# Linear attention in a decoder layer: reciprocals spread by DMA instead of TensorE, and the block's work in another order

## The chip, the cores and the metric

The kernel runs on one core of a Trainium2 chip. The metric is the device time of one execution in microseconds (us), lower is better. Engines are named as in the profile: PE is TensorE, DVE is VectorE, ACT is ScalarE, POOL is GpSimd, SP is SyncE, which here issues the DMAs.

## What is computed

One layer of a decoder on x of shape (2, 2048, 512): linear attention over x, cross attention over a context of 154 rows, and a mixture of experts, each behind a layer norm and added to x. The change touches the linear attention alone. Its mathematics, cut from the reference:

```
x = x + attn(layernorm(x), w_qkv, proj_matrix, w_out, b_out)
q_proj = elu1(einsum('bhnd,hdf->bhnf', q, proj_matrix))
k_proj = elu1(einsum('bhnd,hdf->bhnf', k, proj_matrix))
kv = einsum('bhnf,bhnd->bhfd', k_proj, v)
attn = einsum('bhnf,bhfd->bhnd', q_proj, kv)
k_sum = k_proj.sum(axis=2)
z = 1.0 / (einsum('bhnf,bhf->bhn', q_proj, k_sum) + 1e-08)
out = (attn * z[..., None]) @ w_out + b_out
```

There are 16 heads of 32 columns. The next step of the layer, the query projection of the cross attention, is made in the same stage.

## The kernel before

Tokens are cut into eight blocks of 512 (NBLK = 8). The kernel has four stages: `project` (keys, values and queries), `attend_linear`, `attend_cross` and `experts`. Only `attend_linear` changes; a DRAM array of `attend_cross` moves to the second half of a larger one.

`attend_linear` is a pipeline over the blocks, written out by hand. Each engine runs `turns(slot)`: for i from -1 to 8 and for the slots s = 0 to 7 it does what its own `slot` function lists, in that order. In turn i three blocks are in work: the features of block i+1 ("ahead", two heads in each slot), the division, output projection and layer norm of block i ("now"), and the cross-attention queries of block i-1 ("behind"). What PE does in a slot after the two heads is in the table `PLAN`:

```
0: [("ND", 3), ("XQ", 0, 0, 12)],
1: [("XQ", 1, 0, 12)],
2: [("R", 0), ("R", 1), ("R", 2), ("R", 3), ("XQ", 2, 0, 12)],
3: [("ND", 0), ("O", 0, 0, 12)],
4: [("O", 1, 0, 12), ("O", 2, 0, 6)],
5: [("ND", 1), ("O", 2, 6, 12), ("O", 3, 0, 12)],
6: [("XQ", 3, 0, 12), ("T", 0), ("T", 1)],
7: [("ND", 2), ("T", 2), ("T", 3)],
```

The jobs are these.
- Head h: one matmul (L1166), ACT relu (L1003) and exp (L1006), and DVE's sum of both (L1086), which makes `qp`, ring of eight. PE may run three heads ahead of DVE (three banks `li_h_bank`).
- ND g: denominators (`p_den`, L1176) and numerators (`p_num`, L1182) of four heads. ACT evicts them to `den` (L960) and `num` (L951).
- Reciprocals: two DVE instructions of half a row each (L1049) write `den[:, 1]`; only 16 of the 128 rows hold different numbers. ACT (L965) and POOL (L924) split the reciprocals into a high and a low half.
- R g: two matmuls (L1191) with a constant matrix `spread` copy the reciprocals of four heads to all their 128 rows, in a PSUM bank. DVE multiplies `num` by it (L1054, `normalise`).
- ACT writes the high half of the normalised heads (L971, `normalised`), and POOL the low half of all four groups (L936). The output projection reads both.
- O t: 12 matmuls (L1204) for 128 tokens. Those of t = 0 go group by group, three matmuls each, and each group waits for its low half (`norm_lo`).
- DVE's `add_out` adds an O to x and takes the statistics (L1060 to L1067), POOL takes the power (L942), DVE's `norm` writes `xn` (L1074), which has two buffers, T t is four transposes of it (L1213), and ACT (L980) and DVE (L1080) evict the high and low halves (`turned`).
- XQ g: 12 matmuls (L1226) of the query projection. ACT writes the high half (L989), DVE the low half (L1091), and SP stores both (L874). `xq` has two buffers.

O, T, XQ and R share three PSUM banks in the order of the jobs: a job waits until the third job before it has been evicted (`bank_free`). XQ 0 waits for all four transposes of its block to be evicted. All DMAs are issued by SP, in the order of its own slots, and a wait on SP holds all DMAs behind it.

## Time and profile before

| | |
|---|---|
| time, median of 3 runs | 2378.44 us (2377.59 to 2380.17) |
| time of the profiled execution | 2380.94 us |
| its span | 2379.2 us, 34267 instructions |
| PE busy | 2278.0 us (96%) |
| DVE, ACT, POOL busy | 1390.5, 1158.5, 838.9 us |
| `project` | 0 to 417 us |
| `attend_linear` | 417 to 743.4 us, PE busy 308.66 |
| `attend_cross` | 743.4 to about 1136 us |
| `experts` | about 1136 us to the end |

The limits of the stages were read off the first and last instructions of each. The page's chain of work that ended last names PE for nearly all of its steps, so a stage is worth what happens to PE in it. A "busy" PE may still be running at half clock; the column PEclk of the views by window gives the granted clock as a share of full speed.

### The profile page before, as it was taken

The page shows a single profiled execution, that of the slowest core. Times are in us where ns is not written, and L with a number is a line of the kernel's source. Part 1 is how long each engine was busy: PE and PEld are TensorE (multiplying, and loading weights), DVE is VectorE, ACT ScalarE, POOL GpSimd, SP SyncE. Part 2 cuts the span into 40 slices and gives each one's busy share as a digit, 9 for nine tenths or more (in the row PEclk, how much of TensorE's full clock was granted, in tenths as well). Part 3 has the DMA queues.
Part 4 walks back from the last instruction along what each step waited for, and adds up shares of the span by engine and source line. Part 5 has one row for each costly group of instructions (what it writes and reads, how often), then busy time and mean ns, then how long its engine had stood idle before and what let it go on. Part 6 is the DMA issues. An engine that isn't in the chain of part 4 may idle for free.

```text
span 2379.2 us, 34267 instructions
## 1 busy us (share of the span) xinstructions
PE 2278.0 (96%) x12200; PEld 1775.7 (75%) x12200; DVE 1390.5 (58%) x2258; ACT 1158.5 (49%) x2745; POOL 838.9 (35%) x820
## 2 busy tenths in 40 slices
PE   7999999899998899998799999999999999999998
PEld 6888886566666566665588878888788887888887
DVE  5555456777774668777644466444664445644444
ACT  3555566767663767774544444333343333433332
POOL 1444345333341245545677762111111111111111
PEclk9999999999999899999899999999999999999999
DMA  7655546666646457784656546454345543464442
GB/s 209 161 146 128 134 107 157 210 187 195 177 142 181 102 145 188 185 225 138 217 174 212 177 141 214 171 177 142 129 153 201 177 142 125 136 215 139 140 139 77
DMA packets 140218, 387.46 MB, mean 163 GB/s; under 512 B 15920, under 2 KB 38064, under 8 KB 123440
## 3 DMA queue, kind: packets, MB, share of 16 engines
q1 hardware_dynamic: 139760, 384.77, 53.9%
q8 instruction: 98, 1.61, 0.3%
q10 hardware_dynamic: 288, 0.49, 0.1%
q14 instruction: 72, 0.59, 0.1%
HBM read 254.00 MB, written 104.07 MB: 151 GB/s over the span
## 4 chain that ended last, share of the span: by engine, by line
PE 51%; DVE 1%; issue 0%; ACT 0%; DVEq 0%
PE ex_pg L2593 32%; PE ex_pd L2609 18%; DVE ex_xb L2410 0%; PE ex_pd L2559 0%; PE ex_pd L2570 0%; DVE ex_up L2430 0%; DVE ex_acc L2447 0%; ACT ex_xb L2260 0%; DVE stage L2406 0%; DVE ex_ht L2439 0%; DVE ex_lg L2348 0%; DVE ex_rank L2382 0%; DVE ex_gt L2379 0%; DVE ex_rank L2380 0%; DVE ex_g L2423 0%
## 5 line engine op out<-in xcount | busy, mean ns | idle before, releaser
L2593 PE MATMUL ex_pg<-ex_xb,first_wg 128*128 128x512 f32 x3360 | 821.5, 391 | 12.0 <-DVE ex_up L2430 7.0
L2593 PEld LDWEIGHTS ex_pg<-ex_xb,first_wg 128*128 128x128 f32 x3360 | 632.0, 189 | 153.0 <-issue 15.7
L2609 PE MATMUL ex_pd<-ex_wd,ex_ht 128*128 128x512 f32 x1920 | 486.4, 389 | 2.9 <-issue 2.6
L2609 PEld LDWEIGHTS ex_pd<-ex_wd,ex_ht 128*128 128x128 f32 x1920 | 360.0, 188 | 79.1 <-issue 4.5
L2447 DVE SCALAR_TENSOR_TENSOR ex_acc<-ex_pd,ex_share,ex_acc 128x512 f32<-128x512 f32 x320 | 239.7, 749 | 302.4 <-PE ex_pd L2609 302.2
L2267 ACT COPY ex_m<-ex_pg 128x512 f32<-128x512 f32 x240 | 141.1, 588 | 383.5 <-PE ex_pg L2593 383.4
L2211 POOL TENSOR_TENSOR ex_h<-ex_g,ex_up 128x512 f32<-128x512 f32 x80 | 103.3, 1292 | 553.3 <-issue 458.2
L1590 ACT ACTIVATE cr_prob<-cr_s_bank,cr_top 128x154 f32<-128x154 f32 x512 | 194.7, 401 | 89.3 <-DVE cr_top L1700 86.6
L422 POOL TENSOR_TENSOR pr_ks_sum<-pr_ks_sum,pr_kp 128x512 f32<-128x512 f32 x128 | 165.2, 1291 | 161.6 <-DVE pr_kp L570 150.0
L2271 ACT ACTIVATE ex_g<-ex_g 128x512 f32<-128x512 f32 x160 | 101.3, 633 | 238.0 <-DVE ex_g L2423 165.5
L2203 POOL TENSOR_TENSOR ex_wd<-stage,ex_wd 128x512 fp32r<-128x512 f32 x80 | 105.8, 1343 | 260.1 <-ACT ex_wd L2248 260.1
L2278 ACT CAST ex_ht<-ex_h 128x512 fp32r<-128x512 f32 x160 | 99.4, 622 | 133.1 <-POOL ex_h L2211 133.0
L570 DVE SCALAR_TENSOR_TENSOR pr_kp<-pr_pk,pr_kp 128x512 f32<-128x512 f32 x128 | 88.5, 691 | 104.1 <-ACT pr_kp L475 103.4
L1700 DVE TENSOR_REDUCE cr_top<-cr_s_bank 128x3 f32<-128x462 f32 x192 | 110.4, 578 | 59.3 <-PE cr_s_bank L1865 59.2
L1865 PEld LDWEIGHTS cr_s_bank<-cr_k_w,cr_q 96*128 96x128 f32 x512 | 74.1, 199 | 77.1 <-issue 37.2
L2416 DVE TENSOR_TENSOR ex_g<-ex_pg,ex_m 128x512 f32<-128x512 f32 x80 | 55.3, 691 | 130.1 <-PE ex_pg L2593 124.9
L2439 DVE TENSOR_TENSOR ex_ht<-ex_h,ex_ht 128x512 fp32r<-128x512 f32 x160 | 122.2, 764 | 0.1
L1865 PE MATMUL cr_s_bank<-cr_k_w,cr_q 96*128 96x154 f32 x512 | 98.5, 302 | 20.1 <-DMA cr_q<-xq_scratch 11.9
L1590 ACT ACTIVATION_READ_ACCUMULATOR cr_prob<-cr_s_bank,cr_top 128x1 f32 x512 | 110.1, 215 | 0.0
L1927 PE MATMUL cr_bank<-cr_wo,cr_u 128*128 128x512 f32 x384 | 103.4, 407 | 4.0 <-DVE cr_x L1729 4.0
L1086 DVE SCALAR_TENSOR_TENSOR qp<-li_h_bank,qp 128x512 f32<-128x512 f32 x112 | 75.2, 681 | 46.7 <-ACT qp L1006 46.0
L473 ACT ACTIVATE pr_kp<-pr_pk 128x512 f32<-128x512 f32 x124 | 73.2, 590 | 52.8 <-PE pr_pk L702 52.8
(222 smaller groups left out, 3588.9 us busy)
## 6 DMA issues: line engine op xcount, KB each, us to landing
first_wg<-w_scratch SPq DMA_DIRECT2D x60, 1024.0 KB, 5.1
first_wg<-w_scratch SPq DMA_DIRECT2D x60, 768.0 KB, 4.3
w_scratch<-first_wg SPq DMA_DIRECT2D x20, 1792.0 KB, 6.8
stage<-in_units SPq DMA_DIRECT2D x60, 512.0 KB, 6.9
qk<-pr_kq SPq DMA_DIRECT2D x192, 128.0 KB, 2.4
qk<-q_scratch SPq DMA_DIRECT2D x96, 256.0 KB, 4.7
cr_q<-xq_scratch SPq DMA_DIRECT2D x96, 256.0 KB, 8.0
q_scratch<-pr_kq SPq DMA_DIRECT2D x128, 128.0 KB, 2.3
```

Source lines behind the costliest of these rows:

```text
L422: nc.gpsimd.tensor_tensor(part, part, slot(step), ALU.add).then_inc(ks_step, 1)
L1590: last = nc.scalar.activation(prob[:, n % 2, t, j, 0:KEYS], s_bank[(MU * n + v) % SBANKS][:, at * KEYS:(at + 1) * KEYS], ACT.Exp, bias=top ...
L1700: nc.vector.tensor_reduce(dst.rearrange("p t j -> p (t j)") if t == t_end else dst[:, :, 0], src, AX.X, ALU.max, negate=True).then_inc(top ...
L1865: mm = nc.tensor.matmul(s_bank[at % SBANKS][:, k * KEYS:(k + 1) * KEYS], q3[:, n % QRING, j, t * P:(t + 1) * P], k_w[:, n // G // BLK, j, ...
L1927: mm = nc.tensor.matmul(bank_of("O", m)[:], u[:, s, g, tile_cols(m)], wo[:, w, g], start=(n == 0), stop=(n == 3 * G - 1))
L2203: nc.gpsimd.tensor_tensor(wd[:, n % 2, LO, cols], d_raw[:, cols], wd[:, n % 2, HI, cols].bitcast(F32), ALU.subtract).then_inc(wd_lo, 1)
L2211: nc.gpsimd.tensor_tensor(h[:, f, 1], g[:, f, 1], up[:], ALU.mult).then_inc(h1_set, 1)
L2267: nc.scalar.copy(dst[:], pg[f][BANK[j]][:]).then_inc(m_set, 1)
L2439: nc.vector.tensor_tensor(ht[:, LO, f, k], h[:, f, k], ht[:, HI, f, k].bitcast(F32), ALU.subtract)\
L2447: nc.vector.scalar_tensor_tensor(acc[:, at], bank_of("D", n, i)[:], share[:, NT * half + at, e:e + 1], acc[:, at], ALU.mult, ALU.add).then ...
L2593: mm = nc.tensor.matmul(pg[f][BANK[j]][:], wg[:, f, j, s, c * P:(c + 1) * P], xb[:, j, m, c * TB:(c + 1) * TB], start=(k == 0 and j in FRESH),
L2609: mm = nc.tensor.matmul(bank_of("D", n, i)[:], ht[:, s, f, k, t * P:(t + 1) * P], wd[:, n % 2, m, f * D:(f + 1) * D], start=(at == 0), sto ...
```

## The change

The diff, without the declarations of semaphores and the renamed arguments:

```diff
-        2: [("R", 0), ("R", 1), ("R", 2), ("R", 3), ("XQ", 2, 0, 12)],
-        3: [("ND", 0), ("O", 0, 0, 12)],
-        4: [("O", 1, 0, 12), ("O", 2, 0, 6)],
-        5: [("ND", 1), ("O", 2, 6, 12), ("O", 3, 0, 12)],
-        6: [("XQ", 3, 0, 12), ("T", 0), ("T", 1)],
+        2: [("XQ", 2, 0, 12)],
+        3: [("ND", 0), ("XQ", 3, 0, 12)],
+        4: [("O", 0, 0, 12), ("O", 1, 0, 6)],
+        5: [("ND", 1), ("O", 1, 6, 12), ("O", 2, 0, 12)],
+        6: [("O", 3, 0, 12), ("T", 0), ("T", 1)],
...
-        spread = sb("spread", [P, G, P], F32R)
-        rec = sb("rec", [P, 2, TB], F32R)
+        rec = sb("rec", [P, G, TB])
-        xq = sb("xq", [P, 2, 2, TB], F32R)
+        xq = sb("xq", [P, G, 2, TB], F32R)
...
+                def spread_rec(i):
+                    sp.wait_ge(recip_set, 2 * (i + 1))
+                    for j in range(HG):
+                        sp.dma_start(rec_dram[i, j * G:(j + 1) * G], den[j * HD:j * HD + G, 1]).then_inc(row_out, 16)
+                    sp.wait_ge(row_out, 16 * HG * (i + 1))
+                    if i:
+                        sp.wait_ge(divided, G * i)
+                    rows = rec_dram[i].rearrange("(j g) t -> j g t", j=HG)
+                    for j in range(HG):
+                        sp.dma_start(rec[j * HD:(j + 1) * HD], rows[j:j + 1].broadcast_to([HD, G, TB])).then_inc(rec_in, 16)
...
-                    if behind and s in (1, 2, 3, 7):
-                        query_out(i - 1, (1, 2, 3, 7).index(s))
+                    if now and s == 1:
+                        spread_rec(i)
+                    if behind and s in (1, 2, 3, 4):
+                        query_out(i - 1, s - 1)
...
-                def reciprocal_low(i, n):
-                    cols = slice(n * TB // 2, (n + 1) * TB // 2)
-                    pool.wait_ge(rec_hi, 2 * i + n + 1)
-                    nc.gpsimd.tensor_tensor(rec[:, LO, cols], den[:, 1, cols], rec[:, HI, cols].bitcast(F32),
-                                            ALU.subtract).then_inc(rec_set, 1)
...
-                def reciprocal_high(i, n):
-                    cols = slice(n * TB // 2, (n + 1) * TB // 2)
-                    act.wait_ge(recip_set, 2 * i + n + 1)
-                    nc.scalar.copy(rec[:, HI, cols], den[:, 1, cols]).then_inc(rec_hi, 1)
...
-                    if m or g >= 2:
-                        act.wait_ge(xq_out[g % 2], 16 * (2 * m + g // 2))
+                    if m and g < 2:
+                        act.wait_ge(xq_out[g], 16 * 2 * m)
...
-                    if now and s == 2:
+                    if behind and s == 2:
+                        query(i - 1, 2)
+                    if behind and s == 3:
+                        query(i - 1, 3)
+                    if now and s == 3:
                         for g in range(G):
                             normalised(i, g)
...
-                    dve.wait_ge(r_full, G * i + g + 1)
-                    nc.vector.tensor_tensor(num[:, g], num[:, g], bank_of(i, "R", g)[:], ALU.mult).then_inc(r_taken, 1)
+                    dve.wait_ge(rec_in, 16 * HG * (i + 1))
+                    nc.vector.tensor_tensor(num[:, g], num[:, g], rec[:, g], ALU.mult).then_inc(divided, 1)
...
+                for landed in xq_out:
+                    pool.wait_ge(landed, 16 * NB * BLK * G // 2)
```

The last two lines are POOL's first in `attend_cross`, ahead of two memsets. `spread_rec` has the form that `attend_cross` already uses for its own reciprocals (L1431 to L1440 of the kernel before). DVE's `reciprocal` of a later block also waits until the rows of the block before have left `den`. The low halves of the normalised heads were all on POOL already, and stay there.

On ACT, the place is turn 1, where the first block with queries behind it is divided: end of slot 2, slot 3. `li_xq` is the eviction of an XQ, `li_u_att` the high half of the normalised heads, and the pairs on `qp` are the heads. Before:

```order
L1006 ACTIVATE qp<-qp 128x512
L971 CAST li_u_att<-li_num 128x512 x4
L989 ACTIVATE li_xq<-li_bank,li_bq 128x512
L1003 ACTIVATE qp<-li_h_bank 128x512
L1006 ACTIVATE qp<-qp 128x512
L1003 ACTIVATE qp<-li_h_bank 128x512
L1006 ACTIVATE qp<-qp 128x512
L951 COPY li_num<-li_p_num 128x512
```

After:

```order
L999 ACTIVATE qp<-qp 128x512
L984 ACTIVATE li_xq<-li_bank,li_bq 128x512
L996 ACTIVATE qp<-li_h_bank 128x512
L999 ACTIVATE qp<-qp 128x512
L996 ACTIVATE qp<-li_h_bank 128x512
L999 ACTIVATE qp<-qp 128x512
L984 ACTIVATE li_xq<-li_bank,li_bq 128x512
L966 CAST li_u_att<-li_num 128x512 x4
L952 COPY li_num<-li_p_num 128x512
```

The four casts to `li_u_att` stood ahead of the eviction of XQ 2, and now stand behind that of XQ 3.

On PE, the same place, slots 2 to 4. `li_rec,li_spread` is R, `li_u_ln,wq` is XQ and `li_wo,li_u_att` is O. Before:

```order
L1166 MATMUL li_h_bank<-qk,f_w 128x512 x2
L1191 MATMUL li_bank<-li_rec,li_spread 128x512 x8
L1226 MATMUL li_bank<-li_u_ln,wq 128x512 x12
L1166 MATMUL li_h_bank<-qk,f_w 128x512 x2
L1176 MATMUL li_p_den<-qp,ks_w 32x512 x4
L1182 MATMUL li_p_num<-qp,kv_w 32x512 x4
L1204 MATMUL li_bank<-li_wo,li_u_att 128x512 x12
L1166 MATMUL li_h_bank<-qk,f_w 128x512 x2
L1204 MATMUL li_bank<-li_wo,li_u_att 128x512 x18
```

After:

```order
L1160 MATMUL li_h_bank<-qk,f_w 128x512 x2
L1211 MATMUL li_bank<-li_u_ln,wq 128x512 x12
L1160 MATMUL li_h_bank<-qk,f_w 128x512 x2
L1170 MATMUL li_p_den<-qp,ks_w 32x512 x4
L1176 MATMUL li_p_num<-qp,kv_w 32x512 x4
L1211 MATMUL li_bank<-li_u_ln,wq 128x512 x12
L1160 MATMUL li_h_bank<-qk,f_w 128x512 x2
L1189 MATMUL li_bank<-li_wo,li_u_att 128x512 x18
```

R is gone, and XQ 3, which stood three slots later, stands directly ahead of the heads and the first O.

On DVE, the end of turn 1: from the last `add_out` to the transposes' evictions. Before:

```order
L1060 TENSOR_TENSOR li_x<-li_x,li_bank 128x512
L1062 BN_STATS li_stats<-li_x 128x6
L1064 COPY li_pause<-half 128x1
L1065 BN_AGGR li_mv<-li_stats 128x2
L1067 TENSOR_SCALAR li_mv<-li_mv 128x1
L1086 SCALAR_TENSOR_TENSOR qp<-li_h_bank,qp 128x512
L1074 TENSOR_SCALAR li_xn<-li_x,li_mv,li_rstd 128x512
L1091 SCALAR_TENSOR_TENSOR li_xq<-li_bank,li_bq,li_xq 128x512
L1086 SCALAR_TENSOR_TENSOR qp<-li_h_bank,qp 128x512
L1074 TENSOR_SCALAR li_xn<-li_x,li_mv,li_rstd 128x512
L1080 TENSOR_TENSOR li_u_ln<-li_bank,li_u_ln 128x4x128 x2
```

After, from the first head of slot 6 (`li_xn` is norm):

```order
L1077 SCALAR_TENSOR_TENSOR qp<-li_h_bank,qp 128x512
L1065 TENSOR_SCALAR li_xn<-li_x,li_mv,li_rstd 128x512
L1077 SCALAR_TENSOR_TENSOR qp<-li_h_bank,qp 128x512
L1065 TENSOR_SCALAR li_xn<-li_x,li_mv,li_rstd 128x512
L1051 TENSOR_TENSOR li_x<-li_x,li_bank 128x512
L1053 BN_STATS li_stats<-li_x 128x6
L1055 COPY li_pause<-half 128x1
L1056 BN_AGGR li_mv<-li_stats 128x2
L1058 TENSOR_SCALAR li_mv<-li_mv 128x1
L1071 TENSOR_TENSOR li_u_ln<-li_bank,li_u_ln 128x4x128 x2
L1065 TENSOR_SCALAR li_xn<-li_x,li_mv,li_rstd 128x512
L1077 SCALAR_TENSOR_TENSOR qp<-li_h_bank,qp 128x512 x2
```

The last `add_out` (L1060, now L1051) stood ahead of norm 2, and now stands behind it. The first two evictions of transposes (`li_u_ln`) stood behind norm 3, and now stand ahead of it.

## Rows read from the trace of the kernel before

**Rows 1.** Timeline of PE in turn 3: start, duration, instruction, idle before it.

```profile
539.18 1.06 PE L1176 MATMUL li_p_den<-qp,ks_w 128*32 128x512 f32 x8
...
547.59 1.09 PE L1191 MATMUL li_bank<-li_rec,li_spread 128*128 128x512 f32 x4
...
550.70 3.04 PE L1226 MATMUL li_bank<-li_u_ln,wq 128*128 128x512 f32 x12 [0.46 <-DVE li_num L1054]
...
555.99 3.02 PE L1204 MATMUL li_bank<-li_wo,li_u_att 128*128 128x512 f32 x12
...
559.31 4.29 PE L1204 MATMUL li_bank<-li_wo,li_u_att 128*128 128x512 f32 x18
...
573.30 1.03 PE L1213 MATMUL li_bank<-ident,li_xn 128*128 128x128 f32 x8
...
578.71 1.07 PE L1176 MATMUL li_p_den<-qp,ks_w 128*32 128x512 f32 x8
```

**Rows 2.** Timeline of ACT in turn 3: an eviction of XQ, the high halves.

```profile
544.15 0.69 ACT L989 ACTIVATE li_xq<-li_bank,li_bq 128x512 fp32r<-128x512 f32 x1 [0.58 <-PE li_bank L1226]
...
550.27 1.65 ACT L971 CAST li_u_att<-li_num 128x512 fp32r<-128x512 f32 x3
```

**Rows 3.** Timeline of POOL in turn 3: the four low halves.

```profile
550.95 5.03 POOL L936 TENSOR_TENSOR li_u_att<-li_num,li_u_att 128x512 fp32r<-128x512 f32 x4 [1.36 <-ACT li_u_att L971]
```

**Rows 4.** Timeline of DVE in turn 3: second reciprocal, add_out, norm, evictions.

```profile
543.58 1.74 DVE L1049 RECIPROCAL li_den<-li_den 128x256 f32<-128x256 f32 x1
...
561.24 0.68 DVE L1060 TENSOR_TENSOR li_x<-li_x,li_bank 128x512 f32<-128x512 f32 x1
...
563.02 0.68 DVE L1086 SCALAR_TENSOR_TENSOR qp<-li_h_bank,qp 128x512 f32<-128x512 f32 x1
...
574.01 0.55 DVE L1074 TENSOR_SCALAR li_xn<-li_x,li_mv,li_rstd 128x512 f32<-128x512 f32 x1 [1.20 <-PE li_bank L1213]
...
576.18 1.28 DVE L1080 TENSOR_TENSOR li_u_ln<-li_bank,li_u_ln 128x512 fp32r<-128x512 f32 x2
```

**Rows 5.** Cross stage: landings of broadcasts (L1440), of rows (L1434), four issues.

```profile
DMA to landing us min/median/max: 3.6/5.0/7.3
...
DMA to landing us min/median/max: 1.6/1.6/5.0
...
839.07 1.74 SPq L1440 DMA_DIRECT2D cr_rec<-rec_scratch  x4
```

**Rows 6.** Timeline of DVE and PE in turn 0, the first block.

```profile
429.09 1.74 DVE L1049 RECIPROCAL li_den<-li_den 128x256 f32<-128x256 f32 x1
...
441.97 0.63 PE L1166 MATMUL li_h_bank<-qk,f_w 96*128 96x512 f32 x2
...
453.66 1.04 PE L1213 MATMUL li_bank<-ident,li_xn 128*128 128x128 f32 x8
...
460.15 1.06 PE L1176 MATMUL li_p_den<-qp,ks_w 128*32 128x512 f32 x8 [0.20 <-DVE qp L1086]
```

**Rows 7.** Timeline of PE and DVE in turn 7, the last block.

```profile
697.29 1.07 PE L1176 MATMUL li_p_den<-qp,ks_w 128*32 128x512 f32 x8 [1.05 <-DVE qp L1086]
...
724.64 1.03 PE L1213 MATMUL li_bank<-ident,li_xn 128*128 128x128 f32 x8
...
729.81 11.16 PE L1226 MATMUL li_bank<-li_u_ln,wq 128*128 128x512 f32 x48 [1.49 <-DVE li_u_ln L1080]
...
699.15 3.37 DVE L1049 RECIPROCAL li_den<-li_den 128x256 f32<-128x256 f32 x2 [0.71 <-ACT li_den L960]
```

**Rows 8.** By window: length, busy PE PEld DVE ACT POOL, PEclk, DMA, GB/s.

```profile
432.00:434.00 2.00, 2.00 (x6) 1.49 (x5) 1.24 (x2) 1.97 (x4) 2.00 (x3) 0.50 0.01 0
```

**Rows 9.** Timeline of DVE and POOL: two equal DVE instructions, one beside POOL.

```profile
419.02 2.29 DVE L1132 TENSOR_TENSOR li_wo<-stage,li_wo 128x2048 fp32r<-128x2048 f32 x1 [3.23 <-ACT li_wo L994]
...
441.93 3.05 DVE L1141 TENSOR_TENSOR wq<-stage,wq 128x2048 fp32r<-128x2048 f32 x1 [1.10 <-ACT wq L1011]
...
440.31 2.53 POOL L919 TENSOR_TENSOR li_x<-li_x,li_bias 128x512 f32<-128x512 f32 x2
```

More of the change, by code:

```diff
@@ L1103, in slot @@
                     if s == 6 and now:
-                        add_out(i, 3)
+                        add_out(i, 2)
                     if s == 2 and behind:
                         query(i - 1, 1)
-                    if s == 2 and now:
-                        normalise(i, 0)
+                    if s == 3 and behind:
+                        query(i - 1, 2)
                     first()
```

100 lines of the change are left out of this document (40 added, 60 removed).

## The prediction

> **What bounds the kernel now.** I read the page's chain first: it names PE for nearly every step, so the linear stage is worth the time that PE needs for it. Then I read the timelines of one middle turn, engine by engine. The reader is to see two things in PE's rows. First, a turn repeats after 39.53 us (539.18 to 578.71) [rows 1], and from the first block's end to the last block's start there are six such turns: 697.29 - 460.15 = 237.1 us [rows 6, 7]. Second, PE has hardly a gap in them: the largest, 0.46 us, lies in R's section [rows 1]. So work taken off PE is worth its own time, if nothing new makes PE wait. What has slack in a turn is how early a product is ready before PE wants it. The low halves of the heads are an example: POOL starts them at 550.95 and is done at 555.98 [rows 3], and the first O starts at 555.99 [rows 1]. It waits for the low halves one group at a time, and three of the four are long there. ACT's casts for them start at 550.27 [rows 2], while XQ 2 and an ND still lie ahead of O on PE. That cover is what the change moves.
>
> **R goes from PE.** R starts at 547.59 and XQ 2 at 550.70 [rows 1]: eight matmuls and the gaps between them, 3.1 us in each turn. All of it is on PE's path. ACT and POOL lose the two half splits of the reciprocals, off the path, worth nothing. DVE's multiplication reads SBUF instead of PSUM, at the same size, so I cost it the same.
>
> **The first O now waits for POOL.** PE's slot 3 ends with XQ 3, and slot 4 is two heads and O 0. ACT's slot 3 evicts XQ 3 and only then casts the four high halves. Call the end of XQ 3 on PE E. ACT's eviction starts 0.1 after E (in the trace, XQ 0's eviction followed PE's release after an idle time of 0.58, that is, ACT was waiting for it) and lasts 0.69, overlapping the next by 0.1 [rows 2], so the first cast starts at E + 0.7. POOL followed the first cast by 0.68 (550.27 to 550.95) [rows 2, 3], so it starts at E + 1.4, and its four passes take 5.03 [rows 3]: the last ends at E + 6.4. PE then has three matmuls left of O 0, 0.7 us (12 take 3.02 with the pipeline's tail) [rows 1]. So O 1 starts at E + 7.1. Without waits, two heads and 12 matmuls of O take 3.3 us (555.99 to 559.31) [rows 1], counted from XQ 3's last issue, 0.15 before E: O 1 would start at E + 3.2. The wait is 7.1 - 3.2 = 3.9, with the semaphores some 4.0 us a turn. Nothing covers it: PE executes in order, and the heads of slot 5, ND 1 and everything else are queued behind O 0. POOL's rate sets it, not ACT's: a pass is 5.03 / 4 = 1.26, a cast 0.55 (1.65 for three).
>
> **The tail of a turn.** DVE's last `add_out` now stands behind norm 2, and norm 3 behind two evictions. Counted from the first transpose (573.30): norm 2 starts 0.7 later, as now (574.01) [rows 1, 4], and takes 0.5; `add_out` takes 1.8 (561.24 to 563.02) [rows 4]; two evictions 1.2 (1.28 as recorded); norm 3 0.5: 4.7. T 3 can't start before. The heads 14 and 15 follow on DVE, 1.2 more like the pair of evictions of that size, and ND 3 needs the last: 6.0 with the semaphore. Before it was 578.71 - 573.30 = 5.4 [rows 1]. This costs 0.6.
>
> **The broadcast.** The reciprocals are done 6.1 us into the turn (543.58 + 1.74 - 539.18) [rows 1, 4]. SP issues four row stores; an issue takes 0.43 (1.74 / 4), the last lands 1.3 + 1.6 later; then four broadcasts of 256 KB, whose last lands 1.3 + 3.6 to 5.0 later [rows 5]. That is 13.9 to 15.3 us into the turn, 17.6 with the longest landing, 7.3. XQ 3 stands where O 0 stood: 16.8 us into the turn (539.18 to 555.99), less R's 3.1 [rows 1], that is 13.7, and it ends 3.0 later. So E is 16.7, the first cast is due at 17.4, and DVE must have multiplied for 0.7 by then: the data are wanted by 16.7. In a middle turn the DMAs are hidden, with 1.4 us to spare at the median. Queued behind the new waits on SP are the stores of XQ and loads of queries. With four `xq` buffers no eviction waits for those stores in the same turn, and the loads are for the turn after: nothing.
>
> So a middle turn costs -3.1 + 4.0 + 0.6 = +1.5 us, and six cost **+9.0**.
>
> **First block.** It has no queries behind it, so nothing covers the DMAs. The reciprocals end at 430.83 [rows 6]; 2.9 us for the rows, 6.3 for the broadcasts at the median landing: 440.1. Then 0.7 for DVE, 0.7 for ACT to POOL, 5.0 on POOL, 0.7 on PE: O 0 is through at 447.2, where it was at 441.97 [rows 6]. Later in this turn the tail was 6.5 (453.66 to 460.15) [rows 6] and becomes 6.0. Together **+4.8**.
>
> **Last block.** The reciprocals end at 702.52 [rows 7], and 9.2 us of DMAs end at 711.7, behind XQ 3, which ends near 710.5. By the same steps O 1 starts at 718.8. 36 matmuls take 8.6 (twice 4.29 for 18) [rows 1], so the transposes start at 727.4 instead of 724.64: +2.8. Here no heads or ND stand between the transposes: norm 3 at 4.7, T 3 with ACT's and DVE's evictions 2.0: XQ 0 of the last block follows at 6.8 instead of 5.2 (724.64 to 729.81) [rows 7]: +1.6. Together **+4.4**. POOL's new wait at the start of the cross stage is ahead of memsets for which nobody waits so early: nothing.
>
> **The sum** is 9.0 + 4.8 + 4.4 = +18.2 us. On the profiled execution's 2380.94 that is 2399.1. The median of the runs lies 2.5 lower; on it, 2396.6. I say **2397**.
>
> **Rivals.**
>
> A. The stall grows. Three things could do it. A landing of 7.3 instead of 5.0 [rows 5] costs 0.9 in each of six turns and 2.3 in the two end blocks, +10. PE's clock can fall to its lower level of 1.2 GHz, granted 0.50, as it did after two waits for single heads in the first turn [rows 8]; the new turn has a 2.3 us gap followed by matmuls in small groups. Until it rises, PE's work behind O 0 takes twice its time: 1 to 2 us where it happens, up to +12. And DVE's multiplication now has both inputs in SBUF, as POOL's passes have. In the trace two DVE subtractions of one size, both inputs in SBUF, took 2.29 alone and 3.05 beside a POOL instruction that ended 0.91 into it [rows 9]. If multiplications 2 and 3 hold POOL up by 0.7 each in every block, that is 1.3 x 8 = +10. The Trainium skill states this as a rule ("SBUF — State Buffer", section "Who interferes with whom"): an instruction of DVE with two SBUF inputs and one of GpSimd that reads SBUF exclude each other for their whole length; the trace's one pair agrees. With one of the three in full, 2407 to 2409 (2396.6 and 10 to 12).
>
> B. The stall is hidden and the kernel gets faster. If O 0 found its low halves ready, a middle turn would give -3.1 + 0.6 = -2.5, six -15; the ends would cost about 3 each for their DMAs: 2369. It decides at the casts: they must start 4 us before XQ 3 ends. Against it stands ACT's order, in which the cast follows XQ 3's eviction in every turn that has queries.
>
> C. Things cancel: the wait is 2.5 instead of 4.0 and the tail is free, as if POOL's passes or ACT's start were quicker than the rows have them. Then a turn costs -0.6, and with the ends +9.2 the sum is about +5 or less: 2379 to 2383.
>
> **Chances and range.** My case, 2388 to 2403: 0.60. A, beyond that: 0.26. C: 0.07. B: 0.07. The range takes my case and most of A: 2388 to 2412. Under 0.2% (4.8 us) this kernel's runs can't be told from no change. Faster 0.07, same 0.07, slower 0.86.
>
> **What would show it.** Right: no R; PE waiting for POOL's L936 (now L937) before the O 0 groups, in sum about 2.3 us and then three gaps of 0.5 in each turn; POOL's four passes starting 1.4 after XQ 3's end; turns of 41.0 us instead of 39.53; DVE waiting for the broadcast in the first and last turn only. Wrong: turns under 39.5, or a wait for DMA in the middle turns. It would be wrong at the root if ACT's casts started before XQ 3 ends. A granted clock under 1 in the middle turns would be rival A.

## The result

The changed kernel takes **2415.25 us** (median of 4 runs, 2411.29 to 2416.74), the kernel before 2378.02 beside it: a ratio of 1.0153, interval 1.0135 to 1.0171. Slower, as forecast, but by 37 us where 18 to 19 were forecast, and outside the range. The profiled execution took 2416.28 us, its span is 2414.5.

All of it lies in the linear stage. The times below run from ND 3 to ND 3 in TensorE's timeline, six turns; F is the first block (from the stage's first matmul to the first ND 3 with queries behind it), L the last (from its ND 3 to the first matmul of the cross stage).

| kernel | F | turns 1 to 6 | L | stage |
|---|---|---|---|---|
| before | 43.0 | 39.5 each | 46.2 | 326.4 |
| changed | 53.4 | 48.9, 42.6, 41.2, 41.1, 41.2, 41.2 | 54.2 | 363.8 |

So +10.4 in F, +9.4 in turn 1, +3.1 in turn 2, some +1.6 in each of the other four, +8.0 in L. The stages behind are 3.2 us shorter.

**An undisturbed turn.** The changed kernel, turn 3, all engines in one timeline; start, duration, instruction, idle before it and what ended it. It answers to [rows 1 to 4].

```profile
563.20 1.07 PE L1170 MATMUL li_p_den<-qp,ks_w 128*32 128x512 f32 x8
...
578.10 1.29 DVE L1045 TENSOR_TENSOR li_num<-li_num,li_rec 128x512 f32<-128x512 f32 x2 [0.96 <-DMA li_rec<-rec_scratch]
...
579.85 0.69 ACT L984 ACTIVATE li_xq<-li_bank,li_bq 128x512 fp32r<-128x512 f32 x1 [2.29 <-PE li_bank L1211]
...
580.43 2.16 ACT L966 CAST li_u_att<-li_num 128x512 fp32r<-128x512 f32 x4
581.12 4.99 POOL L937 TENSOR_TENSOR li_u_att<-li_num,li_u_att 128x512 fp32r<-128x512 f32 x4 [7.22 <-ACT li_u_att L966]
...
582.53 6.20 PE L1189 MATMUL li_bank<-li_wo,li_u_att 128*128 128x512 f32 x18 [2.25 <-POOL li_u_att L937]
...
604.38 1.07 PE L1170 MATMUL li_p_den<-qp,ks_w 128*32 128x512 f32 x8
```

R is gone, and TensorE waits 2.25 us for POOL instead. ACT evicts XQ 3 as soon as TensorE has it, then casts, and POOL starts 1.3 us after the eviction's start. Eighteen matmuls took 4.29 before [rows 1] and take 6.20: O 0 follows POOL's pace. Behind the wait the granted clock falls to its lower level, in each of turns 3 to 6. The line has the columns of [rows 8]; PEclk is the third number from its end.

```profile
584.00:586.00 2.00, 2.00 (x6) 1.37 (x5) 1.72 (x3) 1.36 (x3) 2.00 (x2) 0.50 0.40 153
```

**Turn 1.** The same kernel: SP's queue and DVE, then the view by window (length, busy PE PEld DVE ACT POOL, PEclk, share of the DMA engines, GB/s).

```profile
472.66 0.40 SPq L904 DMA_DIRECT2D li_x<-in_x  x1
473.17 0.45 SPq L915 DMA_DIRECT2D stage<-in_WkT  x1
...
477.60 1.30 SPq L883 DMA_DIRECT2D rec_scratch<-li_den  x4
488.01 1.70 SPq L889 DMA_DIRECT2D li_rec<-rec_scratch  x4
...
495.16 1.29 DVE L1045 TENSOR_TENSOR li_num<-li_num,li_rec 128x512 f32<-128x512 f32 x2 [9.55 <-DMA li_rec<-rec_scratch]
```
```profile
476.00:480.00 4.00, 4.00 (x19) 3.28 (x18) 3.05 (x4) 3.10 (x6) 0.13 (x1) 1.00 1.05 384
480.00:484.00 4.00, 4.00 (x24) 2.78 (x26) 2.83 (x5) 3.69 (x7) 2.42 (x2) 1.00 1.05 388
```

Three loads of 1 MB for the next stage (WkT, WvT, WoT) were issued just ahead of the four row stores, behind the load of x, which is 1 MB too and stands there in every turn. The 16 engines are full; the rows, 32 KB together, are through only after 10.4 us, when the broadcast is issued. In turn 3 the same step took 2.4 us.

**Turn 2.** The same kernel, POOL and DVE:

```profile
538.52 6.17 POOL L937 TENSOR_TENSOR li_u_att<-li_num,li_u_att 128x512 fp32r<-128x512 f32 x4 [8.13 <-ACT li_u_att L966]
538.79 2.29 DVE L1129 TENSOR_SCALAR stage<-stage 128x2048 f32<-128x2048 f32 x1
```

The row stores took 2.4 us here as well (526.51 to 528.90). What is different from the turns behind it is a scaling on DVE, of one of the next stage's weights, beside POOL's passes, which take 6.17 us instead of 4.99.

**The first block**, DVE, POOL and PE; it answers to [rows 6]. Then the clock.

```profile
441.61 1.29 DVE L1045 TENSOR_TENSOR li_num<-li_num,li_rec 128x512 f32<-128x512 f32 x2 [4.66 <-DMA li_rec<-rec_scratch]
...
443.03 7.93 POOL L937 TENSOR_TENSOR li_u_att<-li_num,li_u_att 128x512 fp32r<-128x512 f32 x4 [13.06 <-ACT li_u_att L966]
443.42 3.12 DVE L1045 TENSOR_TENSOR li_num<-li_num,li_rec 128x512 f32<-128x512 f32 x2
...
444.44 4.94 PE L1189 MATMUL li_bank<-li_wo,li_u_att 128*128 128x512 f32 x9 [4.74 <-POOL li_u_att L937]
...
446.46 3.37 DVE L1133 TENSOR_TENSOR wq<-stage,wq 128x2048 fp32r<-128x2048 f32 x1
...
451.01 4.21 PE L1189 MATMUL li_bank<-li_wo,li_u_att 128*128 128x512 f32 x9 [1.64 <-POOL li_u_att L937]
```
```profile
448.00:452.00 4.00, 2.37 (x5) 1.40 (x6) 3.03 (x3) 1.91 (x4) 4.00 (x2) 0.50 0.00 0
452.00:456.00 4.00, 4.00 (x10) 2.67 (x8) 1.78 (x5) 0.25 (x1) 1.98 (x3) 0.50 0.00 0
```

DVE's second pair of multiplications takes 3.12 us where the first takes 1.29, and POOL's four passes 7.93 instead of 5.03 [rows 3]. Part of that lies beside the subtraction for `wq` (L1133), which in the kernel before began only behind POOL's passes [rows 9]. **The last block**, PE; it answers to [rows 7].

```profile
729.72 11.17 PE L1211 MATMUL li_bank<-li_u_ln,wq 128*128 128x512 f32 x48
745.50 13.65 PE L1189 MATMUL li_bank<-li_wo,li_u_att 128*128 128x512 f32 x48 [4.60 <-POOL li_u_att L937]
766.23 13.34 PE L1211 MATMUL li_bank<-li_u_ln,wq 128*128 128x512 f32 x48 [1.49 <-DVE li_u_ln L1071]
```

Each of these groups is 48 matmuls. The one ahead of the waits takes 11.17 us, the two behind them 13.65 and 13.34. The first of these two also follows POOL's passes; what the clock costs in each is shown by end_filler below.

### The profile page after: what moved, and what is told of

It reads as the page before. It is cut to its first block, busy times and chain, and to the rows that moved or that the text cites. A ratio compares the mean times of both kernels' runs of the same rounds, so it can differ in the third digit from the quotient of the medians.

```text
span 2414.5 us, 34168 instructions
## 1 busy us (share of the span) xinstructions
PE 2279.0 (94%) x12136; PEld 1773.8 (73%) x12136; DVE 1398.5 (58%) x2257; ACT 1152.9 (48%) x2729; POOL 830.9 (34%) x804
## 4 chain that ended last, share of the span: by engine, by line
PE 50%; DVE 1%; issue 0%; ACT 0%; DVEq 0%
PE ex_pg L2580 32%; PE ex_pd L2596 18%; DVE ex_xb L2397 0%; PE ex_pd L2546 0%; PE ex_pd L2557 0%; DVE ex_up L2417 0%; DVE ex_acc L2434 0%; ACT ex_xb L2247 0%; DVE stage L2393 0%; DVE ex_ht L2426 0%; DVE ex_lg L2335 0%; DVE ex_rank L2369 0%; DVE ex_gt L2366 0%; DVE ex_rank L2367 0%; DVE ex_g L2410 0%
## 5 line engine op out<-in xcount | busy, mean ns | idle before, releaser
L1189 PE MATMUL li_bank<-li_wo,li_u_att 128*128 128x512 f32 x384 | 111.0, 445 | 33.8 <-POOL li_u_att L937 33.7
L1189 PEld LDWEIGHTS li_bank<-li_wo,li_u_att 128*128 128x128 f32 x384 | 78.8, 214 | 67.8 <-issue 40.0
```

Of the source, the lines that this page charges most:

```text
L1189: mm = nc.tensor.matmul(bank_of(i, "O", t)[:], u_att[:, s, g, t * P:(t + 1) * P], wo[:, m, g], start=(n == 0), stop=(n == MM - 1))
```

## The experiments

The measured turns of all of them, as in the table above (us). A kernel's runs lie 3 to 9 us apart, and one run of each was profiled. So an effect of a microsecond or two is read from the turns, and the time can't confirm it. half_bytes leaves out half of each broadcast; it is a test and no candidate.

| kernel | F | turns 1 to 6 | L | time | ratio to before |
|---|---|---|---|---|---|
| w_late | 50.6 | 42.0, 43.7, 41.9, 41.2, 41.4, 41.3 | 54.2 | 2408.10 | 1.0134 |
| scale_late | 50.6 | 42.0, 41.5, 41.5, 41.1, 42.5, 41.7 | 54.9 | 2408.02 | 1.0119 |
| casts_first | 52.0 | 49.8, 43.5, 40.8, 40.7, 40.5, 40.9 | 54.2 | 2411.61 | 1.0140 |
| lock_off | 52.5 | 51.7, 43.6, 42.1, 43.1, 42.2, 43.3 | 55.6 | 2423.56 | 1.0196 |
| reorder_only | 44.6 | 40.0, 40.0, 40.1, 40.0, 40.1, 40.1 | 49.0 | 2387.40 | 1.0040 |
| spread_only | 52.7 | 50.1, 46.1, 43.3, 43.8, 44.1, 44.2 | 53.7 | 2428.91 | 1.0207 |
| filler | 54.2 | 49.2, 42.0, 41.4, 41.2, 41.1, 41.4 | 55.5 | 2416.87 | 1.0150 |
| end_filler | 53.7 | 49.3, 43.6, 41.8, 41.5, 41.2, 41.4 | 52.4 | 2416.98 | 1.0159 |
| best_dve | 50.6 | 40.2, 45.3, 39.6, 40.1, 40.1, 39.9 | 53.4 | 2400.60 | 1.0079 |
| best_split | 50.7 | 41.9, 40.1, 40.0, 39.8, 40.1, 41.7 | 54.0 | 2402.57 | 1.0093 |
| dve_low_only | 51.3 | 41.1, 41.7, 38.8, 39.6, 38.8, 39.7 | 54.3 | 2397.14 | 1.0071 |
| half_bytes | 48.1 | 37.9 each | 52.9 | 2373.97 | 0.9984 |
| split_alone | 50.5 | 41.0 each | 53.3 | 2401.56 | 1.0097 |
| split_bcast | 45.9 | 37.8, 39.6, 37.8, 37.9, 37.8, 37.9 | 48.1 | 2374.03 | 0.9977 |
| r_in_ends | 44.5 | 37.8, 40.0, 37.8, 37.9, 37.8, 37.8 | 49.2 | 2375.58 | 0.9988 |
| weights_by_turn | 45.2 | 37.8 each | 48.1 | 2372.90 | 0.9978 |

### The queue ahead of the rows

```diff
+                    if i == 1 and s == 1:      # behind spread_rec(i)
+                        ...the load of WkT, WvT and WoT
-                    if i == 0 and s == 7:
-                        ...
```

> The changed kernel, with the load of the next stage's three weights (3 x 1 MB on SP's queue) moved from turn 0's slot 7 to turn 1's slot 1, behind the rows and broadcasts of the reciprocals. Theory A (the rows of block 1 stand in SP's queue behind 3 MB of weights, 0.5 MB of x and 1 MB of queries and land 10 us late): turn 1 lasts 41.2 us instead of 48.9, DVE's wait for the broadcast in it falls from 9.6 to about 1 us, and the kernel takes 2407.5 us (7.7 less). Theory B (block 1's turn is long because of something else in it, the clock or the two engines' shared reads; the queue only hides it): turn 1 stays above 46 us and the kernel above 2412.

Turn 1 falls from 48.9 to 42.0, the kernel by 7.1 us. Theory A, with 0.8 us of turn 1 left. (The load of x is 1 MB, not 0.5.) No run tells whether the rows wait for their place in SP's queue or for their share of the 16 engines. Turn 2 stays long, at 43.7, and its timeline shows DVE and POOL side by side:

```profile
527.30 6.45 POOL L937 TENSOR_TENSOR li_u_att<-li_num,li_u_att 128x512 fp32r<-128x512 f32 x4 [8.04 <-ACT li_u_att L966]
527.84 2.29 DVE L1129 TENSOR_SCALAR stage<-stage 128x2048 f32<-128x2048 f32 x1
```

```diff
-                    if i == 2 and s == 3:      # the scaling, L1129
+                    if i == 3 and s == 1:
```

> As w_late, with VectorE's scaling of one of the next stage's weights (128x2048, 2.3 us, in place in SBUF) moved from turn 2's slot 3, where GpSimd makes the low halves, to turn 3's slot 1. Theory A (in turn 2 the scaling holds GpSimd's passes up, which took 6.5 us instead of 5.0 and made O 0 wait in pieces, behind which the clock fell to 0.50 for 6 us): turn 2 lasts 41.3 us instead of 43.7, turn 3 up to 0.5 us more, the kernel 2405.5 to 2407, 1.5 to 2.5 less than w_late. Theory B (turn 2 is long for another reason, for instance the transfers of queries behind the weights): turn 2 stays at 43 to 44 us and turn 3 gets up to 2 us longer, the kernel 2408 or more.

Turn 2 is 41.5, so the scaling beside POOL was its cause. (In split_alone, where the data land sooner, the scaling stays in turn 2, is over at 527.6 as POOL starts at 527.4, and the turn lasts 41.0.) But turn 5 and L are longer by about as much, and the kernel's time is the same as w_late's instead of 1.5 to 2.5 less. In turn 5 the first eighteen matmuls of O took 7.21 us where they took 5.96 in turn 4, and PEclk stood at 0.50 for some 4 us behind the wait instead of 2. Why it did isn't settled.

### The order alone, and the DMAs alone

reorder_only is the kernel before with the changed PLAN, the changed order on DVE and ACT, and four `xq` buffers, R kept:

```diff
-        3: [("ND", 0), ("O", 0, 0, 12)],
+        3: [("ND", 0), ("XQ", 3, 0, 12)],
...
-                    if behind and s == 6:
+                    if behind and s == 3:
                         query(i - 1, 3)
```

> The kernel before, with TensorE's spreading of the reciprocals and GpSimd's and ScalarE's part in it kept, and only the order changed as in the changed kernel: the last block's queries in slots 0 to 3 through four buffers in SBUF, out projection and norms one slot later. Theory A (the order costs only the tail of a turn, 0.6 us, since the multiplications stay in slot 2 and the low halves are ready before O 0): middle turns last 38.3 to 38.6 us, the kernel 2380 to 2385. Theory B (the order alone is what costs, because O 0 comes nearer to ScalarE's work of slot 3 or because the later norms meet the next heads): middle turns above 40 us, the kernel above 2395. Either way the difference to the changed kernel is what spreading by DMA costs in place of TensorE's.

40.06 us a turn, 0.5 above 39.53: the tail, as priced in the prediction. Both theories missed: the turn lies above the 38.3 to 38.6 of A, which don't follow from its own 0.6, and the time below the 2395 of B. In F and L the order costs 1.6 and 2.8. The rest of the change's loss, 27.9 us, comes with the spreading by DMA in this order. spread_only is the other half, the changed kernel with the old order in PLAN and in the slots of ACT, DVE and SP:

```diff
-        3: [("ND", 0), ("XQ", 3, 0, 12)],
+        3: [("ND", 0), ("O", 0, 0, 12)],
...
```

> The changed kernel with the order of the kernel before: the last block's fourth query bank back in slot 6, O 0 in slot 3, VectorE's sums, norms and evictions where they were, so that of the change the spreading by DMA is left, with the multiplications in slot 3. Theory A (XQ 3 ahead of O 0 is what covers the DMAs and half of GpSimd's chain: 3 us): the data land as late as before, O 0 stands 3 us earlier in the turn and waits 3 us longer, less the 0.6 of the tail: middle turns last 43 to 44.5 us against 41.2, the end blocks as in the changed kernel but for the tail, the kernel 2427 to 2435. Theory B (the order gives nothing with the DMAs either, it only costs its tail): middle turns 40.6 to 41.3, the kernel 2408 to 2415.

43.3 to 44.2 in turns 3 to 6: without XQ 3 ahead of it, O 0 waits 4.9 us instead of 2.3. Theory A. The two parts don't add up: beside the DMAs the new order saves 13.7 us, alone it costs 9.

### The chain at O 0, and two engines at SBUF

```diff
+                    if now and s == 3: ...normalised(i, g)
                     if behind and s == 3:
                         query(i - 1, 3)
-                    if now and s == 3: ...normalised(i, g)
```

> The changed kernel, with ScalarE's four casts of the normalised heads placed ahead of its eviction of the last block's fourth query bank instead of behind it. Theory A (a middle turn's 4.0 us at O 0 is the chain eviction of XQ 3, cast, GpSimd's subtraction, first product of O 0, started by that eviction): the chain then starts with DVE's multiplication instead, 1.6 us earlier, O 0 waits about 0.7 to 1 us instead of 2.3 us, a middle turn lasts 39.6 us instead of 41.2, over six turns -9 us, the kernel about 2406. Theory B (the chain is set by the broadcast's landing or by GpSimd, so that an earlier cast finds nothing to cast): middle turns stay at 41.0 to 41.3 us and the kernel within 3 us of 2415.

It gave 0.5 us a turn instead of 1.6, and the kernel 2411.6 instead of 2406. The wait before the first low half fell from 2.3 to 1.2, but behind each group new waits stand, since POOL now starts while DVE still multiplies:

```profile
578.98 5.88 POOL L937 TENSOR_TENSOR li_u_att<-li_num,li_u_att 128x512 fp32r<-128x512 f32 x4 [6.10 <-ACT li_u_att L966]
579.32 3.16 DVE L1045 TENSOR_TENSOR li_num<-li_num,li_rec 128x512 f32<-128x512 f32 x2
580.39 0.93 PE L1189 MATMUL li_bank<-li_wo,li_u_att 128*128 128x512 f32 x3 [1.19 <-POOL li_u_att L937]
...
581.98 0.96 PE L1189 MATMUL li_bank<-li_wo,li_u_att 128*128 128x512 f32 x3 [0.66 <-POOL li_u_att L937]
```

```diff
-                    act.wait_ge(divided, G * i + g + 1)
+                    act.wait_ge(divided, G * (i + 1))
```

> The changed kernel, with ScalarE's first cast waiting for all four of DVE's multiplications (one number in one wait), so that GpSimd's subtractions and DVE's multiplications, both with two operands in SBUF, no longer run at the same time. Theory A (the two engines hold each other up at SBUF: DVE's second pair took 3.1 us instead of 1.3, GpSimd's four 7.9 instead of 5.0 in the first block): the pair takes 1.3 us in every block, GpSimd's four 5.0 us in blocks 0, 2 and 7, the first and the last block are 1 to 2 us shorter each, middle turns as before, the kernel 2410 to 2414. Theory B (the long durations are waits in the engine for something else, such as ScalarE's casts arriving late or the DMA writes): the pair stays near 3 us in blocks 0 and 1, and the kernel within 1 us of 2415 or slower by the later casts, up to 2418.

The pair takes 1.28 us in every block, the first too, and POOL's four 5.0 in the middle turns and the last block. In the first block they still take 6.30 instead of 7.93: the 1.3 above 5.0 lie beside the subtraction for `wq`. That the two engines hold each other up is shown, by three kernels. With one operand in PSUM (before, reorder_only) they overlapped and took 1.28 and 5.03; with both in SBUF and overlapping 3.16 and 5.88; with both in SBUF and apart 1.28 and 5.00. The price expectation failed: the later casts cost more than the lock gave, O 0 waits 3.5 us, and the kernel is 8 us slower. Removing the contention by waiting is worse than having it.

### The clock

```diff
+                        if t == 0 and n == 0:
+                            for _ in range(8):
+                                nc.tensor.matmul(bank_of(i, "O", t)[:], wo[:, HI, 0, 0:P], wo[:, HI, 0], start=True, stop=True)
```

> The changed kernel with eight extra matmuls (128x128 by 128x512, into O 0's own bank, overwritten by O 0's first product) ahead of each block's first O 0 matmul, so that TensorE works through the first 2 us of its wait for the low halves. Theory A (the wait makes the clock fall to 1.2 GHz, granted 0.50, and the matmuls behind it pay): O 0 to O 3 of the last block take 11.5 us again instead of 13.7, the first block's O is through 1 to 2 us sooner, middle turns lose 0.2 to 0.5 us of their 41.2 (there GpSimd's pace holds O 0 anyway), the kernel 2407 to 2411. Theory B (the clock falls for another reason, the fillers only add work): the same windows show 0.50, and the kernel stays within 1 us of 2415 or gets slower by the fillers, up to 2419.

Nothing was gained at the ends: a wait of 3.5 us was left in the last block, and the granted clock behind it was 0.50 again. In turn 3 the clock did stay at 1.00 (580 to 590), and the turn lasted 41.2 as before. So in a middle turn the fallen clock costs nothing that shows: O 0 has to follow POOL at either level. For the ends the filling was made as long as the waits:

> The changed kernel with extra matmuls (128x128 by 128x512, into the bank that the next real product overwrites) only where TensorE waits in the two end blocks: 18 ahead of O 0 of the first and of the last block (4.6 us, the length of the wait there), 9 ahead of T 3 and 5 ahead of XQ 0 in the last block's tail. The eight of the run before covered 2 of these 4.6 us and left a wait of 3.5 us, behind which the clock fell all the same. Theory A (the clock falls because TensorE waits, and would stay at 2.4 GHz if it works on): the last block's O 0 to O 3 take 11.3 us instead of 13.7 and its XQ 0 to XQ 3 11.2 instead of 13.3, the first block gains 0 to 2 us, the linear stage is 4 to 6 us shorter and the kernel 2409 to 2412. Theory B (the fall comes from something else, such as the power drawn by all the work before): the windows show 0.50 as before and the kernel takes 2414 to 2420.

PE in the last block, and two windows of the changed kernel, then the same places here:

```profile
747.31 0.96 PE L1192 MATMUL li_bank<-li_wo,li_u_att 128*128 128x512 f32 x3 [0.61 <-POOL li_u_att L937]
...
768.36 11.18 PE L1220 MATMUL li_bank<-li_u_ln,wq 128*128 128x512 f32 x48 [0.24 <-DVE li_u_ln L1071]
```
```profile
744.00:748.00 4.00, 2.50 (x5) 1.65 (x6) 2.56 (x3) 1.50 (x3) 4.00 (x3) 0.50 0.40 154
...
766.00:770.00 4.00, 3.77 (x9) 3.03 (x10) 0.08 (x1) 0.00 (x0) 0.00 (x0) 0.50 0.01 4
```
```profile
746.00:750.00 4.00, 2.64 (x10) 1.21 (x8) 2.47 (x3) 1.40 (x3) 4.00 (x3) 1.00 0.44 168
...
768.00:772.00 4.00, 3.76 (x17) 3.03 (x17) 0.30 (x1) 0.53 (x1) 0.00 (x0) 1.00 0.00 0
```

The mechanism is shown: with the waits filled the granted clock stays at 1.00, which is 2.4 GHz, and XQ takes 11.18 us instead of 13.34. Its worth was over-rated. O 0 to O 3 were to take 11.3 us; they take 13.3 at full clock (747.31 to 760.61) where they took 13.65, since O 0 follows POOL anyway, and the fillers delay XQ 0. L is 1.8 us shorter, but the stage isn't (364.9 against 363.8, where 4 to 6 less were expected), and the kernel's time didn't move.

### What the wait is made of

Three kernels join the edits of w_late and casts_first with norm 3 ahead of T 1's eviction and with low halves on DVE: all four in best_dve and dve_low_only, two in best_split. best_dve and best_split also have ND 1 ahead of O 0.

```diff
+                        for g in range(G):      # DVE, slot 3, behind normalise(i, 3)
+                            low(i, g)
-        5: [("ND", 1), ("O", 1, 6, 12), ("O", 2, 0, 12)],
+        4: [("ND", 1), ("O", 0, 0, 12), ("O", 1, 0, 6)],
```

> The changed kernel with five edits: the weights' load behind the broadcast (as in w_late), the casts ahead of the eviction of XQ 3 (as in casts_first), all four low halves on VectorE right behind its multiplications instead of on GpSimd, ND 1 of the next block ahead of O 0 instead of behind O 1's first half, and norm 3 ahead of the eviction of T 1. Theory A (the middle turn of 41.2 us is 36.4 us of TensorE's work plus the wait at O 0 and the later tail, and both can be covered): the wait at O 0 vanishes, norm 3's gap too, middle turns last 37.0 to 38.0 us against 39.53 of the kernel before, the first and last block stay 6 to 8 us longer each, the kernel about 2378 to 2384. Theory B (VectorE, with 30 of 41 us busy, becomes the bound once it takes the low halves too, or the broadcast lands too late for the shorter turn): middle turns stay above 39 us and the kernel above 2388.

> As best_dve, but the low halves of groups 0 and 1 on VectorE and those of groups 2 and 3 on GpSimd. Theory A (two operands in SBUF on both engines hold each other up): VectorE's low halves or second pair of multiplications take 1 to 2 us longer than in best_dve, GpSimd's two passes 1.5 us each instead of 1.26, middle turns are the same or up to 0.7 us longer than in best_dve. Theory B (no such lock; sharing out the work is worth it): VectorE's instructions keep their 0.6 us, and middle turns are up to 0.5 us shorter than in best_dve.

> As best_dve, but ND 1 stays behind O 1's first half, where the changed kernel has it. Theory A (the cover ahead of O 0 counts): O 0 finds its first low half some 1 us late, a middle turn lasts 38.5 to 39.5 us, 1 to 1.5 us more than in best_dve, where ND 1's 1.9 us cover it, the kernel 2386 to 2392. Theory B (what counted was GpSimd's rate of 1.26 us a pass alone): middle turns are within 0.3 us of best_dve's.

All three are slower than expected, and for best_dve theory B holds (39.6 to 40.1 us a turn from turn 3 on). ND 1 as cover was an error, and the order of the two kernels came out the other way round: best_dve is 3.5 us slower than dve_low_only (part of it in turn 2, where the broadcast came 4.0 us late). ND 1 waits 1.85 us for ACT's `take_num`, which waits for the low half of the same `num`. In best_split two low halves on DVE beside POOL take 2.36 us instead of 1.28 (theory A), and turns 3 to 5 average 40.0 as in best_dve (39.9). In dve_low_only O 0 still waits 1.6 to 2.4 us, now for a chain that begins with DVE's wait of 0.9 to 1.7 us for the broadcast.

```diff
-                        sp.dma_start(rec[j * HD:(j + 1) * HD], rows[j:j + 1].broadcast_to([HD, G, TB]))
+                        sp.dma_start(rec[j * HD:(j + 1) * HD, 0:G // 2], rows[j:j + 1, 0:G // 2].broadcast_to([HD, G // 2, TB]))
```

> As dve_low_only, but only the first two of each four groups of reciprocals are broadcast (0.5 MB instead of 1 MB a block) and used for all four, which leaves the rest of that part of the computation out; number and kind of instructions are the same. Theory A (the broadcast's landing sets when O 0 can start, and its bytes set the landing: 1 MB at the 200 to 230 GB/s that the windows show is 4.5 to 5 us): VectorE's wait for it shrinks or goes, data are there 2.0 to 2.5 us sooner, the wait at O 0 falls from 1.6 to 2.4 us to under 0.5, middle turns last 37.0 to 37.6 us instead of 38.8 to 39.7, the end blocks are 2 us shorter each, the kernel 2380 to 2386. Theory B (the landing is fixed latency of eight small transfers in two steps behind each other, whatever their size): VectorE's wait stays within 0.5 us of 0.9 to 1.7, middle turns at 38.5 or more, the kernel 2394 to 2399.

Theory A: 37.87 us in every turn, a little more than expected, and the kernel 6 us less. The same number of transfers, of half the size, and DVE no longer waits for them in the middle turns; O 0 waits 0.6 us. All bytes, in two halves, with two of the low halves ahead of the second pair of multiplications:

```diff
+                    for n in range(2):
+                        part = slice(n * G // 2, (n + 1) * G // 2)
                         for j in range(HG):
+                            ...rec[j * HD:(j + 1) * HD, part]... .then_inc(rec_in[n], 16)
```

> As dve_low_only, but the broadcast is made in two halves, first groups 0 and 1 of all heads (four transfers of 128 KB), then groups 2 and 3, each half with its own semaphore, and VectorE makes the low halves of groups 0 and 1 ahead of multiplications 2 and 3. All bytes are moved. Theory A (bytes set the landing, 2.3 us for each half, and O 0 needs groups 2 and 3 only 1.5 us after 0 and 1): the first half lands 2 to 2.5 us sooner, VectorE's first pair no longer waits in middle turns, these last 37.9 to 38.3 us as in half_bytes, F (the first block, 51.8) becomes 49 to 50.5, L (the last, 54.3) 52 to 53.5, the kernel 2378 to 2384. Theory B (the halves are in flight together and share the 16 engines, so the first half lands hardly sooner, and the four issues more on SP's queue delay the second): middle turns stay at 38.8 us or more, the kernel 2394 or more.

Its turn 4 (SP's queue, DVE, PE):

```profile
586.68 3.55 SPq L891 DMA_DIRECT2D li_rec<-rec_scratch  x8
...
591.97 1.28 DVE L1044 TENSOR_TENSOR li_num<-li_num,li_rec 128x512 f32<-128x512 f32 x2
...
593.77 1.29 DVE L1048 TENSOR_TENSOR li_u_att<-li_num,li_u_att 128x512 fp32r<-128x512 f32 x2
...
595.02 1.55 PE L1197 MATMUL li_bank<-li_wo,li_u_att 128*128 128x512 f32 x6
...
597.09 3.05 PE L1197 MATMUL li_bank<-li_wo,li_u_att 128*128 128x512 f32 x12 [0.51 <-DVE li_u_att L1048]
```

DVE waits for no transfer, and O 0 waits 0.5 us instead of 2.25 and POOL's pace. The ends gained more than expected, F 51.3 to 45.9 and L 54.3 to 48.1, and the time is 4 us below the expected range. (The 51.8 in the expectation was a misreading: dve_low_only has 51.3.) This kernel is faster than the one before, 0.9977 (0.9968 to 0.9987).

> As w_late, with the broadcast in two halves and nothing else: the low halves stay on GpSimd, the casts behind the eviction of XQ 3. Against w_late it is the halves alone. Theory A (in middle turns the eviction of XQ 3, the casts and GpSimd's rate set the wait at O 0, so that an earlier landing is worth nothing there; in the end blocks the landing comes first): middle turns stay at 41.0 to 41.4 us, F and L are 1.5 to 3 us shorter each than w_late's 50.6 and 54.2, the kernel 2402 to 2405. Theory B (the late landing is the whole stall, the other four edits of split_bcast were not needed): middle turns fall to 38 to 39 us and the kernel below 2395.

Theory A in the middle: 40.96 to 40.99 us in all six turns. An earlier landing alone is worth 0.2 us there; the chain eviction, cast, POOL had to go too. At the ends the expectation missed: F is 0.1 shorter than w_late's and L 0.9, instead of 1.5 to 3 each. There too the halves gain only together with the low halves on DVE: F is 50.5 with the first alone, 51.3 in dve_low_only and 45.9 in split_bcast.

> As split_bcast, but in the first and in the last block TensorE spreads the reciprocals as in the kernel before (multiplications in slot 2, low halves on GpSimd); blocks 1 to 6 use the DMAs. Theory A (F and L are long because no queries cover the DMAs there, with the fall of the clock behind the wait; nothing else of the change sits in the end blocks but its order, which reorder_only shows at 44.6 and 49.0): F 44.5 to 45.5, L 48.5 to 49.5, middle turns as in split_bcast, 37.9 to 38.3, the linear stage some 321 us against 326.4 of the kernel before and the kernel 2364 to 2371, faster than both. Theory B (the end blocks are long through the lock, the casts or the late first loads, or the change from one way to the other costs what it saves): F above 47 or L above 51, the kernel 2374 or more.

F 44.5 and L 49.2 as expected, but split_bcast has 45.9 and 48.1: with its five edits, DMAs cost the end blocks nothing more than R does. The kernel was expected at 2364 to 2371 and gains nothing over split_bcast (0.9988, 0.9979 to 0.9997). The long ends were the late landing together with POOL's passes, not the DMAs as such.

```diff
+                    if 1 <= i <= 3 and s == 1:      # one weight a turn, behind the broadcast
+                        ...sp.dma_start(staged(stage, i - 1), a[("WkT", "WvT", "WoT")[i - 1]]...)
```

> As split_bcast, with the next stage's three weights loaded one in each of turns 1 to 3, each behind that turn's broadcast, instead of all three in turn 1, and the scaling of one of them in turn 5's slot 1. Theory A (3 MB in turn 1 leave a backlog in the 16 engines which holds up turn 2's row stores: 4.8 us from their issue to the broadcast's issue instead of 2.8): turn 2 lasts 37.8 to 38.2 us instead of 39.6, turns 1, 3 and 4 stay under 38.3, the kernel 2371 to 2373. Theory B (the backlog is there without the weights, or 1 MB does the same in each turn): turn 2 stays above 39, or turns 2 to 4 lose 0.5 us or more each, the kernel 2374 or more.

37.83 us in every turn, turn 2 too. The rows of turn 2 took 4.8 us from their issue to the broadcast's in split_bcast (506.51 to 511.30) and take 2.4 here. Split_bcast first, then this kernel:

```profile
505.16 0.39 SPq L912 DMA_DIRECT2D li_x<-in_x  x1
506.51 1.26 SPq L883 DMA_DIRECT2D rec_scratch<-li_den  x4
...
502.25 0.39 SPq L913 DMA_DIRECT2D li_x<-in_x  x1
...
507.29 1.25 SPq L883 DMA_DIRECT2D rec_scratch<-li_den  x4
509.68 3.55 SPq L891 DMA_DIRECT2D li_rec<-rec_scratch  x8
```

The weights act through the load of x. It waits for the store of the block before, issued at 496.44, which took 8.7 us behind the 3 MB and takes 5.0 here; so x was loaded 1.4 us ahead of the rows instead of 5.0.

This kernel takes 2372.90 us, 0.9978 (0.9969 to 0.9987), 5 us less than before and 42 less than the change. Split_bcast's ratio is the same within the noise; the 1.8 us of turn 2 are seen in the timeline alone.

## Why the prediction was wrong

**What bounds it: right.** TensorE's time is the stage's time. All 37 us stand in its timeline.

**Middle turn: right.** Forecast was a turn of 41.0. Measured 41.1 to 41.2 in turns 3 to 6, and 40.96 in split_alone, where no transfer is late. The wait was forecast as 2.3 us and then O 0 at POOL's pace: 2.25. POOL was forecast 1.4 after XQ 3's end: 1.3 after the eviction's start. The tail, T 0 to ND 3, was forecast as 6.0 and is 5.95 (557.25 to 563.20). One thing I had priced wrongly without harm: the granted clock does fall to 0.50 in each of these turns, my sign for rival A. I had put 1 to 2 us on it; it costs 0.2 at most, since O 0 follows POOL there (filler and split_alone keep 1.00 and have turns of 41.2 and 41.0).

**The broadcast: right in time, wrong in what it claimed.** Forecast to land 13.9 to 15.3 us into the turn, measured 14.9 (578.10 - 563.20). DVE did wait for it, 1.0 to 1.3 us in each of turns 3 to 6, where I said it wouldn't and had called such a wait a sign of being wrong. It is worth 0.2 a turn at most, by split_alone.

**SP's queue: the step that failed.** I listed what is queued behind the new waits on SP and priced it at nothing. I never looked at what stands ahead of the row stores. In turn 1 that is 3 MB of weights, issued under the condition `i == 0 and s == 7`, once in the stage, so that the rows of turn 3 couldn't show it. Turn 1 is 7.7 us longer than the turns behind it, and w_late, which moves only these loads, takes 6.9 of them away. The order of SP's issues was there to be read in the kernel before.

**Turn 2: not in the sum.** Turn 2 is 1.4 us longer, and not by the queue: DVE's scaling of a weight now falls beside POOL's passes, which it holds up by 1.2 us. With the scaling moved away (scale_late) turn 2 is 2.2 us shorter than in w_late. I had looked only for DVE's multiplications beside POOL, not for its other work.

**First block: +4.8 forecast, +10.4 measured, mis-sized.** The landing was sized right (9.3 us from the second reciprocal's end to DVE, forecast 9.2). From the second reciprocal's end (432.3) to O 0's end (some 452.4, a third of the way through the second nine matmuls) it took 20.1 us, forecast 16.4 (430.8 to 447.2). Of the 3.7 us, 2.9 are POOL's four passes, 7.93 instead of 5.03. Some 1.6 of these come with the multiplications and 1.3 with the subtraction for `wq` (7.93, 6.30 in lock_off, 5.0). From there to T 0 (465.74) it took 13.3 us where it was 11.7, which I had left as it was: PEclk is 0.50 up to 456, as in [rows 8]. Rival A named the lock and the clock, each as an addition to the middle turns too; there the lock didn't occur and the clock cost next to nothing.

**Last block: +4.4 forecast, +8.0 measured, mis-sized.** To T 0 it is +3.8 (forecast 2.8), T 0 to XQ 0 7.2 us (forecast 6.8), and XQ 0 to 3 +2.2 at half clock, forecast at nothing.

**The lock** stood in rival A by the Trainium skill, page "SBUF — State Buffer", section "Who interferes with whom": a DVE instruction with two inputs in SBUF contends with a GpSimd instruction that reads SBUF. What the runs show agrees in kind, and gives the price: DVE's pair grows by 1.9 us, POOL's four passes by 0.9 in a middle turn. With the change's own order of casts it doesn't occur there, since DVE's second pair ends as POOL starts (579.91 + 1.28 against 581.12).

**The sum.** Forecast 9.0 + 4.8 + 4.4 = 18.2. Measured in the stage 9.8 (six times 1.64) + 10.4 + 8.0, and 9.2 more in turns 1 and 2: 37.4. The stage began 1.1 later and what follows is 3.2 shorter, so the spans differ by 35.3, the medians by 37.2. Of the 19.2 us missed in the stage, 9.2 are costs that I hadn't looked for (7.7 with the queue, 1.4 with the scaling) and 9.2 lie in the two end blocks, where my durations came from middle turns, with POOL undisturbed and the clock full. That the later stages are 3.2 shorter stays open: it isn't the order, since they are 4.0 shorter in spread_only, which has the old one, and as long as before in r_in_ends, which has the new one. Single runs of a kernel differ by more than that. The range ended 3 us short because rival A was made of one of its three parts, while two of them, at the ends, and the queue came together. Its first part, a late landing, came in turn 1 alone, and not by its landing time.
